# Weight splits of the first tile moved from GpSimd to VectorE, and the gauge scans of the first tile spread over the value projection

## What is computed

```python
xz = x @ Win.T; xi, z = split(xz)                        # 1024 -> 2 x 2048
lam = exp(-8 * softplus(omega) * sigmoid(xi @ Wl.T + bl))  # 2048 x 2048
v   = xi @ Wv.T + bv                                       # 2048 x 2048
h[0] = xi[:, 0]
h[t] = lam[t] * (h[t-1] - 2 v[t] (v[t].h[t-1]) / (v[t].v[t])) + (1 - lam[t]) * xi[t]
y = (silu(z) * h) @ Wout.T                                 # 2048 -> 1024
x = layernorm(x + y)
q = clip(round(x / s), -127, 127) * s
x = layernorm(x + q @ (ternary - 1).T + bias)
```

## Time and profile before

| | us |
|---|---|
| median of the runs (two: 4174.55 and 4516.55) | 4345.55 |
| the profiled execution's own time | 4118.63 |
| its span on the slowest core (core 3) | 4117.0 |
| spans of the eight cores | 4091.3 to 4117.0 |

### The profile page before, as it was taken

The page is one execution under the profiler, slowest core; times in us unless marked ns, Lnnn a source line. Parts: engine busy times, 40 slices in busy tenths (PEclk is TensorE's granted clock), DMA queues, the critical chain, the costliest instruction groups (busy, mean ns, idle before and its releaser), DMA issues.

```text
span 4117.0 us, 53199 instructions; the slowest of 8 cores (4091.3 to 4117.0 us)
## 1 busy us (share of the span) xinstructions
PE 3266.4 (79%) x20764; PEld 2567.4 (62%) x20764; DVE 1254.3 (30%) x2310; ACT 564.0 (14%) x1454; POOL 305.1 (7%) x204
## 2 busy tenths in 40 slices
PE   4855257754898889978997889887997899788965
PEld 3644246631787558854896578755885489657852
DVE  1011512412141332333062214133243306231443
ACT  0001000100121122011111112112201111101211
POOL 0011010200000200020001000020002000010020
PEclk9977677876999899989998899989998999899967
DMA  4444242233552346323642456234633364245602
GB/s 135 142 153 160 81 156 91 88 107 92 174 195 82 111 155 196 113 92 124 207 151 82 133 174 195 82 112 145 204 114 92 124 204 155 82 133 164 194 22 82
DMA packets 171369, 545.28 MB, mean 132 GB/s; under 512 B 20083, under 2 KB 28660, under 8 KB 167028
## 3 DMA queue, kind: packets, MB, share of 16 engines
q1 hardware_dynamic: 163444, 516.72, 39.1%
q0 software_dynamic: 5376, 16.78, 1.2%
q10 hardware_dynamic: 2304, 8.39, 0.5%
HBM read 491.48 MB, written 50.33 MB: 132 GB/s over the span
## 4 chain that ended last, share of the span: by engine, by line
PE 57%; DMA 18%; DVE 10%; issue 5%; ACT 4%; POOL 3%; SPq 1%; DVEq 0%; ACTq 0%; POOLq 0%
PE pb L152 56%; DMA WIN<-w_in 5%; DMA WLV<-wvs 2%; DMA WOU<-wos 2%; DMA WLV<-w_l 1%; DMA WLV<-wls 1%; DVE XFM L756 1%; DMA WLV<-w_v 1%; DMA R<-w_v 1%; DMA R<-w_l 1%; SPq L157 1%; DMA Y<-w_out 1%; DMA WOU<-w_out 1%; DMA WIN<-w_ffn 1%; PE pb L700 1%
## 5 line engine op out<-in xcount | busy, mean ns | idle before, releaser
L152 PE MATMUL pb<-XI,WLV 128*128 128x256 bf16 x11520 | 1304.1, 277 | 116.2 <-DVE WLV L310 26.6
L152 PEld LDWEIGHTS pb<-XI,WLV 128*128 128x128 bf16 x11520 | 1141.0, 99 | 279.3 <-issue 130.1
L152 PE MATMUL pb<-XFM,WIN 128*128 128x256 f32 x4096 | 1016.9, 407 | 124.5 <-DMA WIN<-w_in 73.6
L152 PEld LDWEIGHTS pb<-XFM,WIN 128*128 128x128 f32 x4096 | 824.4, 205 | 290.5 <-issue 164.3
L152 PE MATMUL pb<-WOU,LAM 128*128 128x512 bf16 x1440 | 338.5, 390 | 71.5 <-DVE WOU L850 26.2
L386 DVE TENSOR_TENSOR_SCAN GC<-LAM,ZRO 128x256 f32<-128x256 f32 x128 | 88.6, 692 | 753.9 <-ACT LAM L366 740.4
L152 PEld LDWEIGHTS pb<-WOU,LAM 128*128 128x128 bf16 x1440 | 139.5, 99 | 259.3 <-issue 111.5
L152 PE MATMUL pb<-XI,Y 128*128 128x256 bf16 x768 | 114.7, 324 | 140.1 <-DVE Y L480 78.2
L260 DVE TENSOR_TENSOR XI<-pb,XI 128x256 bf16<-128x256 f32 x128 | 53.6, 423 | 507.9 <-ACT XI L257 507.9
L748 POOL TENSOR_TENSOR KK<-VB,GB 128x512 f32<-128x512 f32 x16 | 44.5, 2780 | 2097.4 <-ACT GB L724 2097.4
L152 PEld LDWEIGHTS pb<-XI,Y 128*128 128x128 bf16 x768 | 87.6, 115 | 167.2 <-issue 144.1
(11 more groups left out here) (177 smaller groups left out, 2236.9 us busy)
## 6 DMA issues: line engine op xcount, KB each, us to landing
WIN<-w_in SPq DMA_DIRECT2D x256, 512.0 KB, 3.7
WLV<-wls SPq DMA_DIRECT2D x224, 512.0 KB, 4.9
WLV<-wvs SPq DMA_DIRECT2D x224, 512.0 KB, 4.9
WOU<-wos SPq DMA_DIRECT2D x224, 256.0 KB, 3.1
XFM<-x_fm POOLq DMA_DIRECT2D x64, 128.0 KB, 7.6
XTM<-x_tm POOLq DMA_DIRECT2D x16, 512.0 KB, 5.1
WLV<-w_l SPq DMA_DIRECT2D x8, 1024.0 KB, 7.5
wls<-WLV SPq DMA_DIRECT2D x16, 512.0 KB, 4.5
```

The costliest lines, as they stand in the source:

```text
L152: return e.matmul(o, l, rr, start=st, stop=sp)
```

## The change

It has two parts, both in tile 0 alone.

1. All splits run on DVE: the three places that chose POOL for some chunks choose DVE for all.
2. In tile 0 the gauge scans are no longer emitted between the lambda and the value projection. A function `emit_gauge_ic(ic)` holds one chunk's six instructions, with one-column memsets of its own chunk for tile 0 (which wait for that chunk's exponentials), and is called once per chunk of the value projection, behind the chunk's split and matmuls. Tiles 1 to 7 call it for all chunks in the old place.

```diff
--- before.py
+++ after.py
@@ -299,8 +299,7 @@
                     wslotb = Y1.bitcast(BF16)[:, 0:2 * N]
                 t_l = dma("sync", slotf, d_wl[jc], "dl%d" % p,
                           waits=(tjsp[p],))
-                jeng = "gpsimd" if jc % 3 == 0 else "vector"
-                jsem = "po" if jc % 3 == 0 else "dv"
+                jeng, jsem = "vector", "dv"
                 t_js = r.do(jeng, lambda e, o=wslotb[:, 0:N], i=slotf:
                             e.tensor_copy(o, i),
                             waits=(t_l, tjmm2[p], tjout2[p], tjsp[p]),
@@ -371,16 +370,19 @@
                               e.activation(o, o, AF.Exp, scale=s),
                               waits=(t_lam[jc],), inc="ac")
 
-        t_ms = None
-        if tile == 0:
-            t_ms = r.do("vector", lambda e: e.memset(fm3(LAM, 0, 1), 1.0),
-                        waits=(t_lam[NIC - 1],), inc="dv")
-            t_ms = r.do("vector", lambda e: e.memset(fm3(KK, 0, 1), 1.0),
-                        waits=(t_lami[NIC - 1], t_ms), inc="dv")
         t_gc = [None] * NIC
         t_rr = [None] * NIC
-        tE = t_ms
-        for ic in range(NIC):
+        tE = None
+
+        def emit_gauge_ic(ic):
+            nonlocal tE
+            t_ms = None
+            if tile == 0:
+                t_ms = r.do("vector", lambda e, o=fm(LAM, ic, 0, 1):
+                            e.memset(o, 1.0), waits=(t_lam[ic], tE), inc="dv")
+                t_ms = r.do("vector", lambda e, o=fm(KK, ic, 0, 1):
+                            e.memset(o, 1.0), waits=(t_lami[ic], t_ms),
+                            inc="dv")
             tE = t_gc[ic] = r.do(
                 "vector", lambda e, o=fm(GC, ic, 0, TT), d0=fm(LAM, ic, 0, TT):
                 e.tensor_tensor_scan(o, d0, ZRO[:, 0:TT], 1.0, AL.mult, AL.add),
@@ -403,6 +405,10 @@
                       waits=(tE, t_s1done, t_xi[ic]), inc="dv")
             tE = r.do("vector", lambda e, o=fm(LAM, ic, 0, TT), i1=rec:
                       e.tensor_mul(o, o, i1), waits=(tE,), inc="dv")
+
+        if tile != 0:
+            for ic in range(NIC):
+                emit_gauge_ic(ic)
         t_bh = tE
 
         t_rb = None
@@ -520,6 +525,8 @@
             wlv_free[sl] = tok
             t_jmm = tok
             tjmm2[jc % 2] = tok
+            if tile == 0:
+                emit_gauge_ic(jc)
             if jc % 2 == 1:
                 for j2 in (jc - 1, jc):
                     tev = r.do("scalar", lambda e, o=fm(VV_, j2, 0, TT),
@@ -529,6 +536,8 @@
                                waits=(tok,), inc="ac")
                     t_v[j2] = tev
                 drain[bank] = tev
+        if tile == 0:
+            t_bh = tE
         if tile == 0:
             split_done["stage"] = split_done["stage"] + (tjsp[1], tjout2[1])
             split_done["wl"] = split_done["wl"] + split_done["wv"] + \
@@ -835,8 +844,7 @@
                     else:
                         slotf = Y1[:, 0:512]
                         wslotb = Y1.bitcast(BF16)[:, 2048:3072]
-                    jeng = "gpsimd" if (dg * NIC + ic) % 4 == 0 else "vector"
-                    jsem = "po" if (dg * NIC + ic) % 4 == 0 else "dv"
+                    jeng, jsem = "vector", "dv"
                     kw = (tjout2[1], tjsp[1]) if wofirst[1] and p == 1 else ()
                     wofirst[p] = False
                     t_l = dma("sync", slotf, d_wo[dg, ic], "wo%d" % p,
```

## The result

| | before | changed |
|---|---|---|
| profiled execution, us | 4118.63 | 4033.82 |
| median of the runs, us | 4290.5 (10 runs, 4169.21 to 4537.01) | 4307.81 (11 runs, 4054.34 to 4455.9) |
| ratio over comparable executions | | 0.9736, 95% interval 0.9616 to 0.9856 |

By the ratio the changed kernel is 2.6% faster, with an interval from 1.4 to 3.8%: it is faster, but whether by more than 2% stays open. Its profiled execution is 84.8 us shorter than that of before. In part of the executions of either kernel the cores of one die, or of both, are granted a lower TensorE clock and take up to 400 us longer; the medians hold as many of these as happened to occur, and the ratio leaves them out. The median of 4307.81 us is outside the predicted range of 4005 to 4115 us.

The account below looks back on a forecast made before the run. In tile 0's projections, load and split in series behind SP's stores were taken as the bound, not TensorE. 14.8 + 12.4 + 5.6 + 2.0 + 57.35 - 3.0 = 89.2 us off 4118.63 gave 4030 us, range 4005 to 4115.

Parts of the forecast that it names:

- Splits in the lambda ring: Lambda projection of tile 0: six POOL splits moved to DVE save 2.47 us each, 14.8 us.
- Splits in the value ring: Value projection of tile 0: five POOL splits after chunk 0 moved to DVE save 2.47 us each, 12.4 us.
- Output ring: Output projection of tile 0: eight POOL splits moved to DVE save 0.70 us each, 5.6 us.
- Gap: Start of the value projection: spreading the gauge scans lets chunk 2's load go out 57.35 us earlier.
- x_fm loads: Tile 1's x_fm loads move to the start and share DMA with the ternary weights' load; 3 us lost.
- Loads behind a POOL split: Lambda and value rings: nine loads issued behind POOL splits looked longer; 2 us taken as won, 5.9 at most.
- Clock in the Gram matrices: Gram matrices from 661 us: granted clock hardly changes, 0 us taken; bounds 6 us shorter, 12 us longer.
- The covers: Value projection: each gauge group fits the 8.6 us between splits, 5 us to spare; without cover, 55 us lost.
- The ring that does not shorten: Tile 0's rings: loads take up what faster splits give, total 4067 us; chance 0.20, wholly or in half.
- The new wait on DVE: Value projection: group 0 waits for all exponentials and later groups delay splits, total 4049 us; chance 0.10.
- The clock that takes it back: Tiles 1 to 7: a granted clock 3% lower costs some 90 us, cancelling the gain; chance 0.05.
- The chances: Whole kernel against a 2% threshold: 0.60 faster, 0.36 within 2%, 0.04 slower.

Follow-up runs that it names:

- part 1 alone: The kernel before with every split on DVE and the gauge scans in their old place; 4123.95 us, beside 4154.0 us for the kernel before.
- the load issued first: The changed kernel with the next chunk's load issued ahead of this chunk's two stores in the lambda and value rings; 3881.3 us in the profiled execution.

## Why the prediction was wrong, and what in it was right

**The step that failed is the basis, not the sum.** The sum was made against the profiled execution, and then I wrote that the median lies 5% above it, that "what is in it besides is not in the trace", and forecast "an execution like the profiled one". The range took in 4085, worked out from the lower of the two runs shown, and left the other out. So the forecast was for one kind of execution and the measured time is a median over two kinds. The evidence was there: of two runs one had taken 4516.55 us with the same instructions, and I used it for a rival with a chance of 0.05. A range for the median had to reach from about 4030 to above 4400 us (4516.55 less the same 89 is 4427), or say that it held only for executions with the clock as profiled. Applied to the 4345.55 us shown, the same 89 us would have given 4256; the median of before itself then moved to 4290.5 and that of the changed kernel was 4307.81. Such a median is not a measure of this change at all: three timings of the two kernels gave 17 us more, 344 us less and 13 us more.

**The sum.** 89.2 us were predicted; the mean core gains 89.1, the profiled execution 84.8, dies at 0.87 or more 85 to 103. That the two first numbers agree to 0.1 us is partly luck: the part behind tile 0 alone scatters by 20 us. What is firm is the 92.8 us up to the first `wls` load, against 87.2 predicted without the 2 us for the loads. By its terms:
- Splits in the lambda ring: 14.8 predicted, 16.7 measured. The duration of the step is right (3.63 us a split), and the kernel with part 1 alone gives 16.3.
- Splits in the value ring: 12.4 predicted, 11.6 measured.
- Output ring: 5.6 predicted, 7.5 measured, of which up to 3.8 may be scatter.
- Gap: 57.35 predicted, 57.6 measured. Load 1 went out 12.59 us behind load 0 (370.75 to 383.34), and 12.59 us had been worked out (386.49 to 399.08).
- x_fm loads: 3 predicted, 2.2 measured at the first w_in load, half of it absorbed before the first w_l load. Holding them back shows the cause.
- Loads behind a POOL split: 2 us were taken, and the term is nothing. The pattern is there with no split on POOL, and over all cores it is 0.4 us a load and not the 0.65 read on one core.
- Clock in the Gram matrices: 0 taken, 0.9 us found in the whole stretch. The bounds given for it (6 us shorter, 12 longer) are too narrow: 39.2 us of TensorE at 0.76 make 29.8 us at 1.00 and 59.6 at 0.50, so 9 shorter and 20 longer as estimates. Nothing came of it.

**The covers.** The prediction said that group 0 would be done 0.9 us before the split can start. It was 1.6 us. It said that each later group fits with 5 us to spare, and three groups in a turn show where the cover ends. That a missing cover would give back what the gap costs was right in kind, with 3.74 us a group in place of 3.46.

**What the prediction didn't see** is the coupling of the two parts. Part 1 pays off fully only with part 2. It costed chunk 0's split in part 2 and never asked what part 1 does alone. With the block in its old place the move to DVE costs 12 us there. In the change as made this has no effect on the sum.

**The rivals.** The ring that does not shorten: refuted, by part 1 alone and more so by the load issued first. The new wait on DVE: not there, since the memsets wait per chunk. The clock that takes it back: the clock does decide what a single execution takes, but behind tile 0 it is 0.93 with and without the change.

**The chances.** The ratio lies outside 2% in its middle, and its interval reaches from 1.4 to 3.8%. The forecast "just above 2%" was the right place, and whether the gain is over 2% is as open as it was.

## What to carry to other kernels

In a ring of load, work and store on one in-order queue, look at what stands ahead of the next load in that queue: here two stores made load and split serial, and putting the load first was worth 152 us where a quicker split had given some 28 in the same two rings. Work that no one needs yet belongs in the time in which its engine waits for a transfer, and the place holds as much as the wait is long. When the ring gets shorter, the same work can be what sets its pace. And count what stands behind it before another split is moved onto the same engine. Before a time is forecast, ask which executions it will be the median of: two runs that differ by 8% say more about the next median than a sum good to a few microseconds.

## What the runs showed of the hardware

- A die's clock can be lower than another's in the same execution, 0.76 to 0.85 in the mean against 0.87 to 0.90, for the same program; the execution is then up to 10% longer. In one profile a stretch without idle time was granted 0.81.
- With two 1 MB loads on the way and the stores between them, the DMA engines of a core moved 286 to 299 GB/s at a share of 0.93 to 1.01 while all eight cores did the same; with one load at a time it was 162 to 173 GB/s.
- The matmuls of one chunk took 7.31 us in the old ring, where TensorE idled between chunks and was granted 0.76 to 0.79, and 5.40 us (351.40 us on core 5's timeline) in the value ring with the load first, at 1.00.
- The loads of three chunks in a cycle are not equal: each third one took 0.3 to 0.4 us longer in five profiles, in the mean of all cores, whichever engine split. No run explains it.
